# Causal mask and row maximum of attention: from mask products on TensorE to one VectorE instruction

## The chip, the cores and the metric

One core of a Trainium2 chip runs a whole decoder layer. The metric is the device time of one execution in microseconds (us). The time before is the median of 3 runs, 1476.31 us (1475.5 to 1485.98). Engines: TensorE (PE) multiplies matrices, VectorE (DVE) does elementwise work and reductions, ScalarE (ACT) activations, GpSimd (POOL) masks and indirect DMAs, SyncE (SP) issues most DMAs.

## The reference

Four batches of 512 tokens of width 512 pass through attention with 16 heads of 32, a quantised linear unit, and a mixture of 16 experts, with a layer norm behind each. What matters here is attention:

```python
scores = jnp.einsum('bsnh,btnh->bnst', k, q) / math.sqrt(HEAD_SIZE)
scores = jnp.triu(scores) + -10000.0 * jnp.tril(ones, k=-1)
attn = jax.nn.softmax(scores, axis=2)
out = jnp.einsum('bnkq,bknh->bqnh', attn, v)
```

It is causal: a query sees the keys up to its own place. The softmax needs, for each query, the largest score over those keys.

## The kernel before

Attention is computed one batch after another, each in a pass over a list of steps written out by hand (`SEQ`, lines 164 to 173). The first pass holds attention of batch 0 alone. Three more passes, a loop, hold attention of batch i merged with the quantised unit and the routing of batch i-1 ("fused passes"). A last pass holds the rest of batch 3 with the first shared-expert tiles (from some 600 us), and after it come the shared and routed experts. Every engine walks the same list, each doing its own part of every step.

The steps of a head h (0 to 15), all with float32 operands:

- `max:h` finds the row maxima. For each block q of 128 queries (4 blocks) PE takes the next of the three banks `psR`, and multiplies 128 queries with their first 256, 256, 384 and 512 keys (line 1171; the narrowest product is 256 wide, of which 128 columns are used). A second product (line 1173) adds the mask of the diagonal block: the identity as weights and a 128x128 bf16 tile `mask_qk` with -1e30 above the diagonal, accumulated on the last 128 columns. It signals `s_rfull`. DVE waits for that and takes the negated maximum over 128, 256, 384 or 512 columns into one column of `nm` (line 1566). Its end signals `s_dfree`, which frees the bank.
- `rows:n`, after each four heads: PE transposes 16 columns of `nm`, DVE splits the result in two parts (lines 1569 and 1571), SP stores them as rows 96 and 97 of `qst` (lines 691 and 692).
- `scores:h` computes the scores transposed, with the negated maxima as two more contraction rows, into `psST`: four products of 512, 256, 384 and 256 columns (line 1185). ACT takes the exponential (line 943), POOL zeroes the masked triangle of the result (line 789). So the causal mask of the output comes from POOL; the mask in `max:h` touches the maximum alone.
- `weigh:h` multiplies by the values and sums the denominators (lines 1202 and 1206).

The three banks `psR` go round in ticket order over all steps that use them: a step may write a bank when the step three tickets ahead has been evacuated, by DVE (`s_dfree`) or ACT (`s_afree`). So a `max` head takes four tickets, and PE can be at most three blocks ahead of DVE. The order around the heads in a fused pass: `max:0 max:1`, two transposes, `max:2`, two transposes, `max:3`, then `xs:0` and `xq:0` (quantisation on DVE, lines 1481 to 1497) beside `qk:4`, `qk:5`, `v:3` on PE; `scores:0` and transposes, then `max:4`, `max:5`, `max:6` with transposes and `scores` between them, `h:0` products, `max:7`; later `max:8` to `max:11`, and `max:12` to `max:15` with `scores:8` to `scores:10` between. The keys and queries of heads 4g to 4g+3 come through a DMA from `scr_d` (line 687), which waits until `scores` of the group two before (4g-8 to 4g-5) has read the same buffer.

POOL builds the constants at the start (lines 738 to 768). PE waits for all 15 of them (line 1098), DVE too.

Of the kernel before, what the change touches and what calls it, by code (L numbers as in the profile page):

```python
# [7 lines left out]
BF16 = mybir.dt.bfloat16  # L8
I32 = mybir.dt.int32
U32 = mybir.dt.uint32  # L10
ALU = mybir.AluOpType
ACT = mybir.ActivationFunctionType
AX = mybir.AxisListType

P = 128
# [6 lines left out]
NEG = -1e30  # L22
BIG = 1e30
# [11 lines left out]
def decoder_layer(nc, x, fside, ctxw, Wqkv, bqkv, Wo, bo, gate_w, ebias, w1, w2, w3, sw1, sw2, sw3, out):  # L35
    B, S, D = x.shape
    C = D // P
    ST = S // P
    I2 = ctxw.shape[2]
    C2 = I2 // P  # L40
    E, _, F = w1.shape
    NT = B * ST
# [13 lines left out]
    with ExitStack() as ctx:  # L56
        def sb(name, shape, dt=F32, stack=ctx):
            return stack.enter_context(nc.sbuf_tensor(name, shape, dt))
# [4 lines left out]
        ident = sb("ident", [P, P])  # L63
        identb = sb("identb", [P, P], BF16)
        ones = sb("ones", [P, P])
        mask_qk = sb("mask_qk", [P, P], BF16)
        hot = sb("hot", [P, 4, 32])
        sel = sb("sel", [P, C, P])
        tri16 = sb("tri16", [P, E, E])
        tri4 = sb("tri4", [P, 4, 4])  # L70
        upper = sb("upper", [P, P])
        k128 = sb("k128", [P, E, NT])
        jrow = sb("jrow", [P, P, 1])
        krow = sb("krow", [P, TOPK, E])
        halfp = sb("halfp", [P, 8])
# [39 lines left out]
        s_rfull = sem("s_rfull")  # L115
# [72 lines left out]
        def apart(eng):  # L188

            eng.sem_inc(s_apart, 1)  # L190
# [141 lines left out]
        nm = sa("nm", [P, HEADS, ST])  # L332
# [395 lines left out]
        def _(pool):  # L728
            n = [0]

            def fill(t, v):
                pool.memset(t, v).then_inc(s_pool_fill, 1)
                n[0] += 1

            def cut(t, pattern, base, mult, op, v):
                pool.affine_select(out=t, in_=t, compare_op=op, fill=v, base=base, pattern=pattern,
                                   channel_multiplier=mult).then_inc(s_const, 1)
            fill(ident[:, :], 0.0)
            fill(identb[:, :], 0.0)
            fill(ones[:, :], 1.0)  # L740
            fill(mask_qk[:, :], 0.0)
            fill(hot[:, :, 0:4], 0.0)
            fill(hot[:, :, 4:32], 1.0)
            fill(sel[:, :, :], 0.0)
# [6 lines left out]
            cut(ident[:, :], [[-1, P]], 0, 1, ALU.not_equal, 1.0)  # L751
            cut(identb[:, :], [[-1, P]], 0, 1, ALU.not_equal, 1.0)

            cut(mask_qk[:, :], [[-1, P]], 0, 1, ALU.is_ge, NEG)
            cut(hot[:, :, 0:4], [[1, 4], [-1, 4]], 0, 0, ALU.not_equal, 1.0)
            for j0 in (0, 2):
                cut(sel[:, :, HD * j0:HD * (j0 + 2)].rearrange("p n (j r) -> p n j r", r=HD), [[-1, C], [-HD, 2], [0, HD]],
# [212 lines left out]
        def _(pe):  # L970
# [135 lines left out]
            def walk(steps, a, b, at):  # L1106
# [6 lines left out]
                for x in steps:  # L1113
# [8 lines left out]
                    kind, n = x[0], (x[1] if len(x) > 1 else None)  # L1122
# [31 lines left out]
                    if kind in ONE:  # L1154
                        t = at.take_bank(pe, x)
# [9 lines left out]
                    elif kind == "max":  # L1165

                        i, j = n // 4 % 2, n % 4
                        for q in range(ST):
                            t = at.take_bank(pe, x, q)
                            w = max(2, q + 1) * P  # L1170
                            pe.matmul(t[:, 0:w], qst[0:96, i, j, q * P:(q + 1) * P], kst[0:96, i, j, 0:w],  # L1171
                                      start=True, stop=False)
                            pe.matmul(t[:, q * P:(q + 1) * P], identb[:, :], mask_qk[:, :], start=False,  # L1173
                                      stop=True).then_inc(s_rfull, 1)
                    elif kind == "rows":
                        mm = pe.transpose(t[0:4 * ST, 0:P], nm[:, 4 * n:4 * n + 4, :].rearrange("p h q -> p (h q)"),
                                          ident[:, :])
                    elif kind == "scores":

                        i, j = n // 4 % 2, n % 4  # L1180
                        for kb in (0, 3, 1, 2):
                            if n and kb in (0, 3):
# [3 lines left out]
                                           start=True, stop=True)  # L1186
                            if kb in (0, 2):
                                mm.then_inc(s_st, 1)
                    elif kind == "weigh":
# [9 lines left out]
                        for kb in ((1, 2, 3) if part else (0,)):  # L1199
# [4 lines left out]
                            for h, j in pair:  # L1204
                                q0 = HD * quad(j)
                                mm = pe.matmul(psDEN[q0:q0 + HD, kb * P:S], hot[:, g, :], pT[:, h % 4, cols],  # L1206
                                               start=(g == 0 and kb == 0), stop=(g == C - 1 and kb == ST - 1),
# [36 lines left out]
        def _(dve):  # L1244
# [196 lines left out]
            def walk(steps, a, b, at):  # L1441
                k = [0]
                asked = [0]
                x = None
# [9 lines left out]
                def done(ins):  # L1454
                    ins.then_inc(s_dfree, 1)
# [79 lines left out]
                for x in steps:  # L1535
                    kind, n = x[0], (x[1] if len(x) > 1 else None)
# [26 lines left out]
                    elif kind == "max":  # L1563
                        for q in range(ST):
                            dve.wait_ge(s_rfull, at.ticket(x) + (q + 1))
                            done(dve.tensor_reduce(nm[:, n, q:q + 1], at.bank(x, q)[:, 0:(q + 1) * P], AX.X, ALU.max,  # L1566
                                                   negate=True))
                    elif kind == "rows":
                        made(dve.tensor_copy(nmh[:, n % 2, :], t[0:4 * ST, 0:P]))
                        after()  # L1570
# [143 lines left out]
```

## Time and profile before

| | us |
|---|---|
| median of 3 runs | 1476.31 |
| lowest, highest | 1475.5, 1485.98 |
| the profiled execution | 1484.92 |
| its span, first to last instruction | 1483.2 |
| TensorE busy in the span | 1339.3 |
| VectorE busy in the span | 888.9 |

The profile shows one execution. Outside the span lie 1.7 us. Durations of matmuls run from start to a modelled end, and successive ones overlap, so what a matmul costs its engine is read from start to start.

### The profile page before, as it was taken

How to read it: one execution, taken by the hardware profiler on the slowest of the kernel's cores; microseconds unless marked ns; L12 is line 12 of the kernel's file. 1: busy time of each engine (PE TensorE's matmuls, PEld its weight loads, DVE VectorE, ACT ScalarE, POOL GpSimd, SP SyncE). 2: the span in 40 equal slices, each digit the busy share in tenths (PEclk: the TensorE clock that was granted, in tenths of full speed). 3: DMA queues.
4: the chain of work that ended last, by engine and by line, in shares of the span. 5: the costliest groups of instructions: out<-in, count | busy, mean ns of one | idle time of the engine just before them, and what ended most of it. 6: DMA issues, size and time to landing. Idle time of an engine off the chain costs nothing.

```text
span 1483.2 us, 24661 instructions
## 1 busy us (share of the span) xinstructions
PE 1339.3 (90%) x7339; PEld 992.9 (67%) x7339; DVE 888.9 (60%) x1579; ACT 411.6 (28%) x627; POOL 389.5 (26%) x478
## 2 busy tenths in 40 slices
PE   7988998999998998789978998999999999879991
PEld 3553455445454455278857887999999999768890
DVE  2542787669856887687757876334343455555634
ACT  1132133303341144212120013223222334343423
POOL 1131012200230014000001671344444344343432
PEclk9989998999989999889998999999999999999996
DMA  8431533225420632413110012645464456868437
GB/s 283 133 89 39 156 92 96 72 87 141 114 72 23 176 100 68 154 39 131 58 57 29 29 37 66 167 77 139 77 141 75 84 133 140 236 175 237 83 72 249
DMA packets 90109, 163.96 MB, mean 111 GB/s; under 512 B 8544, under 2 KB 29536, under 8 KB 89968
## 3 DMA queue, kind: packets, MB, share of 16 engines
q1 hardware_dynamic: 73168, 122.88, 26.7%
q0 software_dynamic: 16816, 39.59, 14.4%
q8 instruction: 57, 0.93, 0.3%
q14 instruction: 68, 0.56, 0.1%
HBM read 113.42 MB, written 49.02 MB: 110 GB/s over the span
## 4 chain that ended last, share of the span: by engine, by line
PE 68%; DVE 11%; DMA 7%; issue 7%; ACT 2%; SPq 1%; POOL 1%; DVEq 1%; ACTq 0%; POOLq 0%
PE psUA L1001 13%; PE psUB L1001 12%; PE psR L1095 11%; PE psY L1008 9%; PE psR L1008 5%; PE psR L1171 3%; PE psOT L1202 3%; PE psST L1185 3%; PE psTX L984 2%; PE psR L1109 2%; DMA kst<-scr_d 2%; PE psTH L1017 2%; DMA room<-in_L_ffn_w_dram 2%; DMA qst<-nml 1%; DVE nm L1566 1%
## 5 line engine op out<-in xcount | busy, mean ns | idle before, releaser
L1001 PE MATMUL psUA<-w_s,xgT 128*128 (+1 forms) x1284 | 244.6, 341 | 18.8 <-DVE xgT L1379 16.1
L1001 PEld LDWEIGHTS psUA<-w_s,xgT 128*128 128x128 f32 x1284 | 214.4, 196 | 27.0 <-DVE xgT L1379 15.4
L1001 PE MATMUL psUB<-w_s,xgT 128*128 (+1 forms) x1284 | 225.3, 324 | 0.0
L1001 PEld LDWEIGHTS psUB<-w_s,xgT 128*128 128x128 f32 x1284 | 211.4, 190 | 0.0
L827 POOL DMA_INDIRECT sx_d<-yg,dst_i x74 | 119.4, 1614 | 299.3 <-ACT yg L905 261.8
L867 ACT ACTIVATE silg<-psUA 128x352 f32<-128x352 f32 x107 | 49.6, 464 | 432.8 <-PE psUB L1001 432.8
L1008 PE MATMUL psY<-w_s,hgT 128*128 (+3 forms) x621 | 163.6, 408 | 0.1
L789 POOL TENSOR_SCALAR_AFFINE_SELECT pT<-pT 128x128 f32<-128x128 f32 (+1 forms) x192 | 68.5, 375 | 347.6 <-ACT pT L943 347.5
L1388 DVE SCALAR_TENSOR_TENSOR hg<-silg,cws,psUB 128x352 f32<-128x352 f32 x75 | 43.5, 579 | 174.4 <-ACT silg L867 174.4
L1566 DVE TENSOR_REDUCE nm<-psR 128x1 f32<-128x128 f32 (+3 forms) x256 | 113.1, 486 | 41.9 <-PE psR L1173 37.5
L1008 PEld LDWEIGHTS psY<-w_s,hgT 128*128 128x128 f32 (+1 forms) x621 | 114.6, 192 | 23.0 <-DVE hgT L1396 0.5
L1095 PE MATMUL psR<-xT,room 128*128 128x512 f32 x256 | 116.9, 603 | 2.5 <-ACT xT L915 2.5
L1394 DVE CAST hgT<-psTH 128x384 fp32r<-128x384 f32 x107 | 59.5, 556 | 93.7 <-PE psTH L1017 93.2
L814 POOL DMA_INDIRECT xg<-x_d,src_i x77 | 98.3, 1277 | 54.1 <-issue 22.2
L943 ACT ACTIVATE pT<-psST 128x512 f32<-128x512 f32 (+1 forms) x128 | 84.3, 703 | 89.3 <-PE psST L1185 88.0
L1171 PE MATMUL psR<-kst,qst 96*128 96x256 f32 (+2 forms) x256 | 94.3, 439 | 16.2 <-DMA kst<-scr_d 6.5
L1259 DVE TENSOR_TENSOR w_s<-room,w_s (+2 forms) x54 | 88.2, 1668 | 32.3 <-ACT w_s L858 29.8
L1095 PEld LDWEIGHTS psR<-xT,room 128*128 128x128 f32 x256 | 48.0, 193 | 59.2 <-issue 54.2
L1202 PE MATMUL psOT<-pT,v_s 128*32 128x256 f32 (+3 forms) x512 | 81.1, 443 | 7.3 <-POOL pT L789 7.3
L1008 PE MATMUL psR<-w_s,hgT 128*128 (+1 forms) x333 | 86.8, 405 | 0.8 <-issue 0.8
L858 ACT CAST w_s<-room (+2 forms) x54 | 73.6, 1404 | 46.6 <-DMA room<-in_L_ffn_w_dram 20.1
L1206 PE MATMUL psDEN<-pT,hot 128*32 128x256 f32 (+3 forms) x512 | 80.9, 443 | 0.0
(218 smaller groups left out, 1901.3 us busy)
## 6 DMA issues: line engine op xcount, KB each, us to landing
room<-in_L_ffn_w_dram SPq DMA_DIRECT2D x32, 704.0 KB
scr_d<-qhl SPq DMA_DIRECT2D x32, 512.0 KB, 3.7
qst<-scr_d SPq DMA_DIRECT2D x48, 256.0 KB, 4.0
kst<-scr_d SPq DMA_DIRECT2D x48, 256.0 KB, 5.9
room<-in_L_ffn_w_dram SPq DMA_DIRECT2D x16, 512.0 KB
xt<-in_x_dram SPq DMA_DIRECT2D x5, 1024.0 KB, 7.2
xr<-in_x_dram SPq DMA_DIRECT2D x4, 1024.0 KB, 5.5
breg<-in_fside_BxS2xS_dram SPq DMA_DIRECT2D x4, 1024.0 KB, 7.1
```

The source lines that it names most:

```text
L814: pool.indirect_dma_start(xg[:, 1 + par, :], None, x2_d, bass.IndirectOffsetOnAxis(ap=src_i[:, j:j + 1], axis=0)).then_inc(s_gat[par], 16)
L827: pool.indirect_dma_start(sx_d, bass.IndirectOffsetOnAxis(ap=dst_i[:, j:j + 1], axis=0), yg[:, par, :], None, compute_op=ALU.add).then_inc ...
L858: act.copy(hi, raw).then_inc(s_whi, 1)
L943: act.activation(pT[:, h % 4, lo:hi], psST[:, lo:hi], ACT.Exp, scale=SCALE).then_inc(s_exp, 1)
L1001: mm = pe.matmul(t[:, 0:F], xgT[:, par, a_, c * P:(c + 1) * P], w[:, buf, b_, c, :], start=(c == 0 and n == 0), stop=(c == C - 1 and n == ...
L1008: mm = pe.matmul(psy[:, :], hgT[0:kn, a_, k * P:(k + 1) * P], w2_s[0:kn, buf, b_, k, :], start=(first and k == 0 and n == 0), stop=(last_ ...
L1095: mm = pe.matmul(out_, l, r, start=(n == 0), stop=(n == len(pairs) - 1))
L1171: pe.matmul(t[:, 0:w], qst[0:96, i, j, q * P:(q + 1) * P], kst[0:96, i, j, 0:w], start=True, stop=False)
L1202: pe.matmul(psOT[HD * j:HD * (j + 1), kb * P:S], v_s[:, kb, h * HD:(h + 1) * HD], pT[:, h % 4, cols], start=(kb == 0), stop=(kb == ST - 1) ...
L1206: mm = pe.matmul(psDEN[q0:q0 + HD, kb * P:S], hot[:, g, :], pT[:, h % 4, cols], start=(g == 0 and kb == 0), stop=(g == C - 1 and kb == ST ...
L1259: dve.tensor_tensor(lo, raw, hi.bitcast(F32), ALU.subtract).then_inc(s_wlo if n in UP else s_w2lo, 1)
L1566: done(dve.tensor_reduce(nm[:, n, q:q + 1], at.bank(x, q)[:, 0:(q + 1) * P], AX.X, ALU.max, negate=True))
```

## The change

The masking product on TensorE goes. VectorE adds a mask row and takes the maximum in one instruction, `tensor_tensor_reduce`: out = (scores + mask) * -1, written back over the scores in the same PSUM bank, and its minimum, started at 1e30, into `nm`. That is the same negated maximum. The mask is now `mask_row`, 512 columns of bf16: zeros with the triangle in the last 128, read from the right end for the width that the block needs. Ahead of each of these instructions `apart(dve)` issues an instruction that only counts up a semaphore, so that the wait for PE sits on that one. To make room, two small constant tables (`tri16`, `k128`) become bf16. The widths, banks, tickets and order of the steps stay.

```diff
-        mask_qk = sb("mask_qk", [P, P], BF16)
+        mask_row = sb("mask_row", [P, ST * P], BF16)
-        tri16 = sb("tri16", [P, E, E])
+        tri16 = sb("tri16", [P, E, E], BF16)
-        k128 = sb("k128", [P, E, NT])
+        k128 = sb("k128", [P, E, NT], BF16)
...
-            fill(mask_qk[:, :], 0.0)
+            fill(mask_row[:, :], 0.0)
...
-            cut(mask_qk[:, :], [[-1, P]], 0, 1, ALU.is_ge, NEG)
+            cut(mask_row[:, S - P:S], [[-1, P]], 0, 1, ALU.is_ge, NEG)
...
                             pe.matmul(t[:, 0:w], qst[0:96, i, j, q * P:(q + 1) * P], kst[0:96, i, j, 0:w],
-                                      start=True, stop=False)
-                            pe.matmul(t[:, q * P:(q + 1) * P], identb[:, :], mask_qk[:, :], start=False,
-                                      stop=True).then_inc(s_rfull, 1)
+                                      start=True, stop=True).then_inc(s_rfull, 1)
...
                             dve.wait_ge(s_rfull, at.ticket(x) + (q + 1))
-                            done(dve.tensor_reduce(nm[:, n, q:q + 1], at.bank(x, q)[:, 0:(q + 1) * P], AX.X, ALU.max,
-                                                   negate=True))
+                            apart(dve)
+                            t = at.bank(x, q)[:, 0:(q + 1) * P]
+                            done(dve.tensor_tensor_reduce(t, t, mask_row[:, S - (q + 1) * P:S], -1.0, BIG, ALU.add, ALU.min,
+                                                          nm[:, n, q:q + 1]))
```

## Rows read from the trace of the kernel before

**Rows 1.** The page: busy time by engine, the chain, the group of the maxima

```profile
PE 1339.3 (90%) x7339; PEld 992.9 (67%) x7339; DVE 888.9 (60%) x1579; ACT 411.6 (28%) x627; POOL 389.5 (26%) x478
...
PE 68%; DVE 11%; DMA 7%; issue 7%; ACT 2%; SPq 1%; POOL 1%; DVEq 1%; ACTq 0%; POOLq 0%
...
L1566 DVE TENSOR_REDUCE nm<-psR 128x1 f32<-128x128 f32 (+3 forms) x256 | 113.1, 486 | 41.9 <-PE psR L1173 37.5
```

**Rows 2.** Groups by form (busy us, mean ns of one | idle before): TensorE's mask product

```profile
L1173 PE MATMUL psR<-mask_qk,identb 128*128 128x128 bf16 x256 | 62.7, 245 | 0.0
```

**Rows 3.** Timeline of TensorE, first pass (start us, length us): one head, then scores

```profile
60.48 0.28 PE L1171 MATMUL psR<-kst,qst 96*128 96x256 f32 x1
...
61.56 0.23 PE L1173 MATMUL psR<-mask_qk,identb 128*128 128x128 bf16 x1
61.60 0.89 PE L1185 MATMUL psST<-qst,kst 98*128 98x512 f32 x4
62.32 0.28 PE L1171 MATMUL psR<-kst,qst 96*128 96x256 f32 x1
```

**Rows 4.** Timeline of TensorE, second pass, at the lower clock

```profile
251.72 1.52 PE L1185 MATMUL psST<-qst,kst 98*128 98x512 f32 x4
253.04 0.41 PE L1171 MATMUL psR<-kst,qst 96*128 96x256 f32 x1
...
255.06 0.63 PE L1109 MATMUL psR<-identb,xq 128*128 128x128 bf16 x4
...
256.77 0.42 PE L1171 MATMUL psR<-kst,qst 96*128 96x256 f32 x1
```

**Rows 5.** Groups by form, VectorE: two widths of the maximum, two kinds with two inputs

```profile
L1566 DVE TENSOR_REDUCE nm<-psR 128x1 f32<-128x512 f32 x64 | 43.7, 683 | 1.2
...
L1557 DVE SCALAR_TENSOR_TENSOR qhl<-psR,bqk,qhl 128x512 fp32r<-128x512 f32 x32 | 23.9, 747 | 35.5 <-ACT qhl L933 35.5
...
L1566 DVE TENSOR_REDUCE nm<-psR 128x1 f32<-128x128 f32 x64 | 18.5, 289 | 33.1 <-PE psR L1173 32.2
...
L1562 DVE TENSOR_TENSOR v_s<-psR,room 128x512 f32<-128x512 f32 x16 | 11.0, 686 | 14.2 <-PE psR L1095 14.2
```

**Rows 6.** Timeline of VectorE: four of its smallest instructions

```profile
744.82 0.38 DVE L1467 BATCH_NORM_AGGREGATE mv<-bn 128x2 f32<-128x6 f32 x4
```

**Rows 7.** Timeline of VectorE: maxima in the first pass and in the second

```profile
59.03 5.42 DVE L1566 TENSOR_REDUCE nm<-psR 128x1 f32<-128x128 f32 x12
...
182.11 3.61 DVE L1566 TENSOR_REDUCE nm<-psR 128x1 f32<-128x128 f32 x8
186.27 1.73 DVE L1566 TENSOR_REDUCE nm<-psR 128x1 f32<-128x128 f32 x4 [0.55 <-PE psR L1173]
...
190.44 2.29 DVE L1481 TENSOR_TENSOR xs<-x,psR 128x2048 f32<-128x2048 f32 x1 [0.16 <-PE psR L1095]
...
205.43 1.73 DVE L1566 TENSOR_REDUCE nm<-psR 128x1 f32<-128x128 f32 x4 [0.32 <-PE psR L1173]
```

**Rows 8.** The chain of waits (start us, us, what) ahead of head 12, second pass

```profile
241.22 6.66 DMA kst<-scr_d
```

**Rows 9.** Timeline of VectorE right behind that

```profile
248.49 1.97 DVE L1566 TENSOR_REDUCE nm<-psR 128x1 f32<-128x128 f32 x5 [1.88 <-PE psR L1173]
```

**Rows 10.** Busy time by stretch: us, engines (instructions), PEclk granted, DMA share, GB/s

```profile
38.98:42.39 3.41, 3.09 (x18) 1.92 (x16) 3.33 (x10) 0.00 (x0) 0.00 (x0) 1.00 0.53 163
42.39:49.22 6.83, 6.83 (x16) 3.63 (x17) 3.53 (x8) 0.00 (x0) 0.00 (x0) 0.50 0.91 214
...
182.34:189.17 6.83, 6.14 (x43) 4.01 (x43) 5.57 (x15) 2.15 (x4) 0.00 (x0) 1.00 0.53 184
250.61:260.85 10.24, 10.24 (x41) 7.61 (x40) 6.36 (x12) 3.88 (x6) 4.36 (x8) 0.50 0.00 1
...
568.40:578.60 10.20, 9.84 (x63) 6.67 (x67) 8.72 (x20) 4.97 (x8) 4.95 (x11) 1.00 0.01 2
```

**Rows 11.** Timeline of GpSimd at the start: a fill of 512 columns

```profile
1.54 0.53 POOL L732 MEMSET sel<- 128x512 f32 x1
```

## The prediction

> **What bounds the kernel now.** Start with the page. TensorE is busy for 90% of the span, VectorE for 60%, and the chain that ended last runs on TensorE for 68% and on VectorE for 11% [rows 1]. So a product taken from TensorE looks like time won. But the change touches only the 64 `max` heads (4 batches, 16 heads), all before 577 us, and there the shares are others. Two questions decide, head by head: how long is a head on TensorE, how long on VectorE, and which of the two do the three banks make the other wait for. The timelines answer that.
>
> TensorE, warm: the head at 60.48 ends where `scores` starts, at 61.60: 1.12 us for eight products. `scores`, four products of 1408 columns, takes 61.60 to 62.32: 0.72 us [rows 3]. The head's four score products also have 1408 columns, so four mask products cost 1.12 - 0.72 = 0.40 us, 0.10 each, though each is shown with 245 ns [rows 2]: products overlap, and only starts count. At the lower clock the head takes 253.04 to 255.06 = 2.02 us and `scores` 1.32: four masks are 0.70 us [rows 4].
>
> VectorE: four maxima are 4 x 486 ns = 1.94 us of busy time [rows 1], but stand in 1.73 us from the first start to the last end [rows 7]: three overlaps of 0.07. Back to back a head takes VectorE 1.94 - 4 x 0.07 = 1.66 us. That is more than TensorE's 1.12. Measured, twelve maxima with `scores` between their heads take 5.42 us, 1.81 a head [rows 7], against 1.12 + 0.72 = 1.84 of TensorE: both engines are nearly full. Two heads back to back take 3.61 us, 1.80 a head; TensorE has time left there and waits for banks, VectorE is the bound. Where two transposes stand between, the next head waits 0.55 us for a bank and its first product. So in much of the `max` work VectorE already sets the pace, and it is VectorE that gets dearer.
>
> **The change, part by part.**
>
> *Taken off TensorE.* 256 mask products with their weight loads: 256 x 0.10 = 26 us if all were on the path and warm. That is the most the change can give, 1.7% of the time (a little more with the three cold stretches). Where VectorE is the bound it gives only latency: the score product now signals itself, and the data are ready sooner by something below the 0.10 us that a mask costs. I take 0.07.
>
> *Added on VectorE.* The trace has no instruction with two inputs and a reduction, and none that writes PSUM. Call d what one of the 256 adds, start to start. By the nearest rows: with 512 columns out of PSUM the maximum shows 683 ns, an add of two inputs 686, a three-operand instruction 747 [rows 5]. So a second input costs nothing, a second operation with a scalar 0.06. If the per-partition result is written by a further small instruction, four of the smallest take 0.38 us, below 0.10 each [rows 6]. Low end: d = 0, if it streams as a plain reduction; below nothing is excluded, since it reads and writes more. Middle: 0.06 + 0.06 = 0.12. High end: between 128 and 512 columns the maximum grows from 289 to 683 ns [rows 5], 1.03 ns a column; the mean width is 320, and if reading and writing one bank made each column cost twice, d would be 0.33. I take d = 0.12, the value nearest to the rows of instructions that do the same arithmetic.
>
> The Trainium skill ("VectorE: DVE Perf Modes", section "Two Vector instructions with no wait between them") says that an operation which also writes out its accumulator is two instructions, the main one and an accumulator read. No row here shows one. By that rule rival 1 below would fall, and the time would be the forecast's or more; it speaks against this change.
>
> *The counting instruction ahead of it* does no work on the engine. While VectorE is behind, TensorE's signal has long come, and the busy instruction before covers it. Where VectorE waits for a head's first block it can add up to 0.1 us (by [rows 6]). Behind it on VectorE stand only the maxima that would have waited too. I set it off against the 0.07 us won above.
>
> *Head by head.* With d = 0.12 a head takes VectorE 1.66 + 0.48 = 2.14 us, TensorE 0.72. Now VectorE is the bound of nearly every `max` stretch.
>
> First pass. Heads 0 to 3, back to back: 1.66 to 1.80 becomes 2.14 twice, the two at the lower clock gain a little: +0.5. Heads 4 to 7, pace 1.84: two steps of +0.3, the one with `weigh` gains 0.2: +0.4. Heads 8 to 11: `max` and other TensorE work mixed, -0.3. Heads 12 to 15: 12 to 13 back to back, +0.4; the other two have a cold TensorE in front of an idle VectorE, 0.7 and more won each with the masks: -1.2 in all with the 0.4. Sum -0.6.
>
> Each fused pass. Heads 0 to 3 stand ahead of the large VectorE work of `xs:0` at 190.44 [rows 7]; VectorE is busy 5.57 of 6.83 us there [rows 10] and the holes of 0.55 are waits for a bank that VectorE itself frees, so they stay. 16 x 0.12 = 1.9, less 0.1 of bank wait that closes between the back-to-back heads, less three holes shortened by 0.07: +1.5. Heads 4 to 6: VectorE idles 0.32 a head [rows 7], 0.48 added: a step of 2.07 becomes 2.14, with head 7 and what `h:0` behind it takes up, +0.2. Heads 8 to 11: TensorE wins some, VectorE loses some, and at the end the load of the next keys (6.66 us [rows 8]) covers both: VectorE idles 1.88 us before head 12 [rows 9]. Here 0. Heads 12 to 15: in passes two and three at the lower clock (0.50 from 250.61 to 260.85 [rows 10]). The pace is 256.77 - 253.04 = 3.73 us [rows 4], far above 2.14, so the 0.70 goes in full three times, less 0.4 at 12 to 13: -1.7. In pass four the clock is 1.00 [rows 10], and there the pace is set near 2.2 either way: 0. Sums: 0, 0, +1.7.
>
> *Start.* The filled mask is 512 columns wide; such a fill took 0.53 us [rows 11], the old one less, and PE waits for all constants: +0.3. The two bf16 tables are used a few times in all: nothing.
>
> Together -0.6 + 0 + 0 + 1.7 + 0.3 = +1.4, taken as +2 with some waits of the counting instruction. The profiled execution took 1484.92 and would take 1487. It stands 8.6 us above the median of 1476.3, so for a median I forecast 1478.
>
> **How it hangs on d.** Up to 0.12 about 105 of the 256 sit where each adds its own d (27 in a fused pass, 24 in the first); above it nearly all bounds move to VectorE, 130 or more. So d = 0 gives 1478 - 105 x 0.12 = 1465; d = 0.3 gives 1478 + 130 x 0.18 = 1501.
>
> **Rivals.**
>
> 1. *The new instruction streams as the old one* (d at most 0.03). For it: the second input is free by [rows 5]. Against: the per-partition result and the scalar operation. Time 1465 to 1469.
>
> 2. *The new instruction is slow* (d from 0.23). One mechanism: it reads and writes the same bank, or waits for its own end before the result is written. VectorE then needs 2.6 to 3.0 us a head, `max` becomes the slowest step of every pass, and heads 8 to 11 outgrow the cover of 1.88 us [rows 9]. For it: no row shows a VectorE write into PSUM. Against: no two-input row is slower than a copy. It decides from d = 0.23, where 130 x 0.11 = 14 us come on top. At 0.33: 1478 + 27 = 1505.
>
> 3. *The clock.* The granted clock was 1.00 in 38.98 to 42.39, when TensorE did back-to-back heads with waits, and 0.50 from 42.39 on; a similar stretch in the second pass, 182.34 to 189.17, kept 1.00 [rows 10]. With the mask products gone and VectorE slower, TensorE streams 1408 columns a head instead of 1920, in longer time,, and could fall to 0.50 in each pass, also in 568.40 to 578.60, which was warm [rows 10]. The price: a pace of 3.73 instead of some 2.2 cost 1.5 us a head for about three heads; one more such stretch in the fourth pass and a shorter one behind heads 0 to 3 of each fused pass make 4.5 + 3 x 1.2 = 8 us: 1486. Against: while VectorE bounds, a slow TensorE costs nothing. The skill's page "TensorE: Matmul & The Clock Gate" (section "What's actually happening") says that the default state is throttled and activity releases it; by that rule work taken away can slow what is left. The fall at 42.39 agrees, the stretch in the second pass shows that it need not come.
>
> **Chances.** Forecast (d 0.05 to 0.2, 1471 to 1488) 0.42; rival 1: 0.17; rival 2: 0.26; rival 3: 0.15. One per cent, 15 us, is about what a measurement of this kernel tells from no change. Faster by over 1% needs d near 0 and a warm clock, half of rival 1 and a little of the rest: 0.13. Slower by over 1%: rival 2 and some of rival 3: 0.30. Same: 0.57. Range 1463 to 1506: rival 1 and rival 2 to d = 0.33.
>
> **What would show it.** The group of the maxima keeps 256 instructions, and its mean rises from 486 to about 550 to 610 ns; above 720 is rival 2. TensorE has 256 products fewer, a warm head takes 0.72 us from its start to `scores`. In 181 to 190 us VectorE's idle falls and `xs:0` starts some 1.5 us later after the pass's start; in the cold stretches the pace falls from 3.73 to about 3.0. TensorE's idle time behind `nm` grows. The forecast is wrong if the heads 4 to 6 keep a pace under 1.9 us (then d is small), or if the row of clocks shows 0.50 in new places.

## The result and the profile after

The change made the kernel slower. Four runs of it have a median of 1507.41 us (1501.98 to 1510.09), against 1475.9 us for four of the kernel before: a ratio of 1.0194, 95% interval 1.0141 to 1.0248 (it is the ratio of the means, 1506.7 and 1478.0; the medians alone give 1.021). The same kernel run again later, six runs against 23, gave 1505.47 against 1481.56 us, 1.0156 (1.0126 to 1.0185). So the change costs 1.6 to 1.9%.

| us | before | after |
|---|---|---|
| median | 1475.9 | 1507.41 |
| the profiled execution | 1484.92 | 1507.82 |
| its span | 1483.2 | 1506.1 |
| TensorE's mean granted clock | 0.954 | 0.934 |

The page of after, the same three lines as in [rows 1]:

```profile
PE 1351.6 (90%) x7075; PEld 990.2 (66%) x7083; DVE 902.3 (60%) x1835; ACT 412.7 (27%) x627; POOL 393.3 (26%) x478
...
PE 67%; DVE 12%; issue 8%; DMA 6%; ACT 3%; POOL 1%; SPq 1%; DVEq 1%; ACTq 1%; POOLq 0%
...
L1566 DVE CUSTOM_DVE_ANT_0 psR<-psR,mask_row 128x128 f32<-128x128 f32 (+3 forms) x256 | 121.5, 513 | 43.5 <-PE psR L1171 40.8
```

TensorE lost its 256 products (7339 to 7075 records, a few are missing) and is still busy 12 us longer; more of its products ran at the lower clock, where a score product of 256 columns is shown with 0.41 us and not 0.28 ([rows 3], [rows 4]). VectorE gained 256 instructions and only 13 us. Neither share of busy time says where 23 us went.

To see where, cut the span at the four reciprocals of the denominators, one at the end of each attention pass: 123.21, 280.44, 440.64 and 596.74 us before, 124.38, 286.62, 454.24 and 621.32 after. Busy time by stretch, with columns as in [rows 10], of before and then of after:

```profile
0.00:123.21 123.21, 108.44 (x568) 57.96 (x568) 42.96 (x87) 31.70 (x48) 26.91 (x83) 0.92 0.53 163
123.21:280.44 157.23, 143.50 (x753) 76.73 (x754) 110.15 (x214) 44.14 (x69) 26.26 (x56) 0.96 0.33 95
280.44:440.64 160.20, 148.06 (x765) 77.32 (x764) 120.50 (x238) 46.22 (x72) 26.19 (x56) 0.96 0.34 96
440.64:596.74 156.10, 143.81 (x765) 74.10 (x764) 119.76 (x238) 45.84 (x72) 26.48 (x56) 0.99 0.34 97
```

```profile
0.00:124.38 124.38, 105.93 (x504) 54.09 (x504) 45.58 (x151) 31.70 (x48) 27.27 (x83) 0.93 0.54 162
124.38:286.62 162.24, 145.16 (x687) 75.22 (x690) 113.25 (x278) 44.36 (x69) 26.76 (x56) 0.92 0.32 92
286.62:454.24 167.62, 152.65 (x699) 76.77 (x700) 123.79 (x302) 46.46 (x72) 26.37 (x56) 0.90 0.32 95
454.24:621.32 167.08, 151.59 (x699) 75.89 (x700) 124.37 (x302) 46.38 (x72) 26.36 (x56) 0.91 0.31 88
```

The passes grew by 1.2, 5.0, 7.4 and 11.0 us, 24.6 together, and what follows took 886.5 us before and 884.8 after. The loss is all in attention, and in the three fused passes the granted clock fell from 0.96, 0.96 and 0.99 to 0.92, 0.90 and 0.91.

**What the new instruction costs.** Groups by form, VectorE, after (busy us, mean ns of one | idle before), beside [rows 5]:

```profile
L1566 DVE CUSTOM_DVE_ANT_0 psR<-psR,mask_row 128x512 f32<-128x512 f32 x64 | 46.1, 721 | 1.1
...
L1566 DVE DVE_READ_ACCUMULATOR2_ANT nm<- 128x1 f32 x256 | 35.8, 140 | 0.3
...
L1566 DVE CUSTOM_DVE_ANT_0 psR<-psR,mask_row 128x128 f32<-128x128 f32 x64 | 19.6, 306 | 34.5 <-PE psR L1171 34.4
```

It is two instructions: a main one of 306 to 721 ns (289 to 683 before) and 256 accumulator reads of 140 ns that write `nm`. The Trainium skill says so ("VectorE: DVE Perf Modes", section "Two Vector instructions with no wait between them"), and this trace agrees. What it costs VectorE is read where nothing waits. Timeline of after, VectorE, first pass:

```profile
62.82 0.60 DVE L1566 CUSTOM_DVE_ANT_0 psR<-psR,mask_row 128x384 f32<-128x384 f32 x1
...
63.33 0.14 DVE L1566 DVE_READ_ACCUMULATOR2_ANT nm<- 128x1 f32 x1
63.33 0.73 DVE L1566 CUSTOM_DVE_ANT_0 psR<-psR,mask_row 128x512 f32<-128x512 f32 x1
...
63.98 0.14 DVE L1566 DVE_READ_ACCUMULATOR2_ANT nm<- 128x1 f32 x1
64.08 0.30 DVE L1566 CUSTOM_DVE_ANT_0 psR<-psR,mask_row 128x128 f32<-128x128 f32 x1
```

The accumulator read of one block lies beside the main instruction of the next: both start at 63.33. From start to start the 384 columns take 0.51 us here. Over all back-to-back pairs the shortest such steps, by width, were 0.197, 0.330, 0.463 and 0.597 us before, and 0.206, 0.349, 0.482 and 0.616 after. So d, what one block adds to VectorE's throughput, is 0.01 to 0.02 us.

What it costs a wait is something else. Timelines of before and then of after, the first block of head 4 in the second pass:

```profile
202.50 0.23 PE L1173 MATMUL psR<-mask_qk,identb 128*128 128x128 bf16 x1
...
202.77 0.29 DVE L1566 TENSOR_REDUCE nm<-psR 128x1 f32<-128x128 f32 x1 [0.55 <-PE psR L1173]
```

```profile
206.38 0.37 PE L1171 MATMUL psR<-kst,qst 96*128 96x256 f32 x1
...
206.94 0.30 DVE L1566 CUSTOM_DVE_ANT_0 psR<-psR,mask_row 128x128 f32<-128x128 f32 x1 [0.75 <-PE psR L1171]
207.16 0.14 DVE L1566 DVE_READ_ACCUMULATOR2_ANT nm<- 128x1 f32 x1
```

Before, the product ends at 202.73 and VectorE starts 0.04 us later; its bank is free at 203.06, 0.29 after the start. After, the product ends at 206.75, VectorE starts 0.19 later, and the bank is free when the accumulator read is over, at 207.30, 0.36 after the start. The signal that frees the bank hangs on the accumulator read in this trace. Over the 256 blocks the least start behind the end of the block's product is 37 ns before and 189 ns after. VectorE waited so for TensorE in more than the first block of a head: 136 of the 256 maxima of before start within 0.06 us of their product's end, and 103 of after within 0.20. The median from start to free bank goes from 291, 424, 549 and 681 ns (by width) to 358, 492, 640 and 788. A block that TensorE and VectorE hand to each other takes 0.15 + 0.07 = 0.22 to 0.15 + 0.11 = 0.26 us longer to come back. The table of waits shows TensorE waiting for banks (what waits <- for what: us in all, times, longest; gaps under 0.15 us are not in it). Of before, then of after:

```profile
PEld psR L1171 <- DVE nm L1566: 11.2, 30, 1.1
```

```profile
PEld psR L1171 <- DVE nm L1566: 38.3, 88, 1.7
```

Not all of this rise is a loss. The experiments below have 25.9 us in this row with the mask product gone and nothing else changed (e1), 31.3 with the counting instruction too (e5), and 12.0 with the counting instruction and the product (e3).

### The profile page after: what moved, and what is told of

It reads as the page before. It is cut to its first block, busy times and chain, and to the rows that moved or that the text cites. A ratio compares the mean times of both kernels' runs of the same rounds, so it can differ in the third digit from the quotient of the medians.

```text
span 1506.1 us, 24653 instructions
## 1 busy us (share of the span) xinstructions
PE 1351.6 (90%) x7075; PEld 990.2 (66%) x7083; DVE 902.3 (60%) x1835; ACT 412.7 (27%) x627; POOL 393.3 (26%) x478
## 4 chain that ended last, share of the span: by engine, by line
PE 67%; DVE 12%; issue 8%; DMA 6%; ACT 3%; POOL 1%; SPq 1%; DVEq 1%; ACTq 1%; POOLq 0%
PE psUA L1001 13%; PE psUB L1001 12%; PE psR L1095 12%; PE psY L1008 8%; PE psR L1008 4%; PE psR L1171 4%; PE psOT L1200 3%; PE psST L1183 3%; PE psR L1109 3%; PE psTX L984 2%; PE psTH L1017 2%; DMA room<-in_L_ffn_w_dram 2%; DMA kst<-scr_d 2%; DMA qst<-nml 1%; DVE w_s L1257 1%
## 5 line engine op out<-in xcount | busy, mean ns | idle before, releaser
L1566 DVE CUSTOM_DVE_ANT_0 psR<-psR,mask_row 128x128 f32<-128x128 f32 (+3 forms) x256 | 121.5, 513 | 43.5 <-PE psR L1171 40.8
L1095 PE MATMUL psR<-xT,room 128*128 128x512 f32 x256 | 123.2, 630 | 2.4 <-ACT xT L915 2.4
L1200 PE MATMUL psOT<-pT,v_s 128*32 128x256 f32 (+3 forms) x512 | 85.8, 464 | 7.4 <-POOL pT L789 7.4
L1171 PEld LDWEIGHTS psR<-kst,qst 96*128 96x128 f32 x256 | 50.2, 222 | 62.7 <-DVE nm L1566 38.3
```

The costliest lines, as they stand in the source:

```text
L1095: mm = pe.matmul(out_, l, r, start=(n == 0), stop=(n == len(pairs) - 1))
L1200: pe.matmul(psOT[HD * j:HD * (j + 1), kb * P:S], v_s[:, kb, h * HD:(h + 1) * HD], pT[:, h % 4, cols], start=(kb == 0), stop=(kb == ST - 1) ...
L1566: done(dve.tensor_tensor_reduce(t, t, mask_row[:, S - (q + 1) * P:S], -1.0, BIG, ALU.add, ALU.min, nm[:, n, q:q + 1]))
```

## The experiments

Three things changed at once: the mask product went, a counting instruction came, and the maximum became the fused instruction. The first runs ask what each does alone, the later ones what the clock has to do with it. Runs e1 to e4 shared one chip, e5 to e8 a second and e9 to e12 a third, each beside runs of the kernel before; from one group to another only the ratios are compared. The ratios are not taken from the medians, and differ by up to 0.2% from the quotients of the medians.

| run | median us (lowest to highest) | ratio to before (95%) | us of attention at 0.50 |
|---|---|---|---|
| e1_product_gone | 1481.19 (1475.91 to 1487.32) | 0.999 (0.9964 to 1.0017) | 75 |
| e3_count_before | 1492.89 (1486.06 to 1499.1) | 1.0071 (1.0041 to 1.01) | 68 |
| e5_gone_count | 1489.96 (1481.92 to 1496.2) | 1.0065 (1.0032 to 1.0099) | 75 |
| e2_both | 1508.4 (1506.04 to 1516.17) | 1.0172 (1.0119 to 1.0225) | 92 |
| e4_filler_ahead | 1507.47 (1495.65 to 1509.69) | 1.0148 (1.008 to 1.0217) | 89 |
| e6_warm_before | 1480.79 (1473.51 to 1491.77) | 1.0011 (0.9986 to 1.0036) | 31 |
| e7_warm_gone | 1480.83 (1476.53 to 1490.73) | 1.0006 (0.9983 to 1.0029) | 62 |
| e8_warm_after | 1503.33 (1502.24 to 1505.34) | 1.0158 (1.0129 to 1.0187) | 79 |
| e9_short_filler | 1481.82 (1466.45 to 1487.98) | 0.9986 (0.9958 to 1.0014) | 48 |
| e10_gone_filled | 1476.94 (1471.38 to 1484.36) | 0.9962 (0.9941 to 0.9982) | 41 |
| e11_after_again | 1505.47 (1500.89 to 1514.89) | 1.0156 (1.0126 to 1.0185) | 126 |
| e12_after_filled | 1500.9 (1496.26 to 1511.4) | 1.0125 (1.0082 to 1.0168) | 72 |

The last column adds up the stretches at a granted clock of 0.50 before the last reciprocal, in each run's profile; it is 51 us in the kernel before and 109 in the profile of after.

### The parts alone

**e1_product_gone**: the kernel before without the mask product; the maximum is the plain one. It leaves the mask out of the maximum alone (a row's maximum is then taken over the whole diagonal block); e5, e7 and e10 leave out the same.

```diff
-                                      start=True, stop=False)
-                            pe.matmul(t[:, q * P:(q + 1) * P], identb[:, :], mask_qk[:, :], start=False,
-                                      stop=True).then_inc(s_rfull, 1)
+                                      start=True, stop=True).then_inc(s_rfull, 1)
```

> The kernel before without the mask product, VectorE's plain maximum kept (the mask is left out of the maximum alone; POOL still masks the result). Clock theory (TensorE with fewer columns between its waits is granted the lower clock, and that is where the 31 us went): the gain of up to 26 us is eaten by cold stretches, granted clock 0.945 or lower, time 1470 to 1490. VectorE theory (the new instruction and its start are the cost): no such cost here, so the products' time comes out as won, 1460 to 1468, clock near 0.954.

Measured: 0.999, and a mean granted clock of 0.946 over the ten runs against 0.955 over those of before. This is about what the clock theory had stated (0.945 or lower, 1470 to 1490 us); the VectorE theory's 1460 to 1468 us did not come. Taking 256 products away gives nothing that can be told from nothing. One reason stands in the table of waits of e1, beside the 11.2 us of before:

```profile
PEld psR L1171 <- DVE nm L1564: 25.9, 71, 1.5
```

TensorE is done sooner and waits for the bank that VectorE frees: this wait grew by 15 us, where the products could give 26 at most. The other reason is the clock: in the profile the second pass has 13.7 us at 0.50 in both kernels and is 3.9 us shorter in e1 (153.37 against 157.23), while the fourth has 20.5 us at 0.50 against 3.4 and is 4.3 us longer (160.38 against 156.10). The section on the clock puts a size on it.

**e2_both**: the kernel after, with a second product of zeros on TensorE, so that its work is that of before.

```diff
                             pe.matmul(t[:, 0:w], qst[0:96, i, j, q * P:(q + 1) * P], kst[0:96, i, j, 0:w],
-                                      start=True, stop=True).then_inc(s_rfull, 1)
+                                      start=True, stop=False)
+                            pe.matmul(t[:, q * P:(q + 1) * P], identb[:, :], mask_row[:, 0:P], start=False,
+                                      stop=True).then_inc(s_rfull, 1)
```

> The changed kernel with a second product kept on TensorE, identity times a tile of zeros, in the place of the mask product; VectorE does the fused instruction. Clock theory: TensorE streams what it did before, the clock is back at 0.95, time 1480 to 1490. VectorE theory: VectorE is as in the changed kernel and TensorE has more to do, 1505 to 1515.

Measured: 1.0172, where the kernel after had 1.0194 and 1.0156, and within what the VectorE theory had stated. The product's return cannot be told from nothing at these intervals (half a per cent either way), so the loss is there with VectorE's part alone.

**e3_count_before**: the kernel before, with the counting instruction ahead of each maximum. **e5_gone_count**: the same in e1.

```diff
                             dve.wait_ge(s_rfull, at.ticket(x) + (q + 1))
+                            apart(dve)
                             done(dve.tensor_reduce(nm[:, n, q:q + 1], at.bank(x, q)[:, 0:(q + 1) * P], AX.X, ALU.max,
                                                    negate=True))
```

> The kernel before with the counting instruction ahead of each plain maximum. It prices the later start of VectorE alone: if the instruction behind a wait of its own starts 0.1 us later, it shows where VectorE waits for TensorE. VectorE theory: a good part of the loss, 1484 to 1492. Clock theory: near nothing by itself, 1476 to 1481, clock 0.95.

> The first experiment (mask product gone, plain maximum; the mask is left out of the maximum) with the counting instruction ahead of each maximum: all that the changed kernel does but the fused instruction itself. Start-latency theory (the counting instruction costs most): 1492 to 1504, near the changed kernel. Fused-instruction theory (a second small instruction and the later release of the bank): 1483 to 1491, so that the fused instruction makes the larger half of what separates it from the changed kernel.

Measured: e3 1.0071 over before, and e5 1.0065 / 0.999, 0.75% above e1. An instruction that does no work and shows no busy time costs 10 to 11 us, the lower clock that comes with it included (0.951 in e3, 0.955 before). Timeline of e3, the same block as above:

```profile
209.45 0.23 PE L1173 MATMUL psR<-mask_qk,identb 128*128 128x128 bf16 x1
209.83 0.29 DVE L1567 TENSOR_REDUCE nm<-psR 128x1 f32<-128x128 f32 x1 [0.72 <-PE psR L1173]
```

The product ends at 209.68, VectorE starts at 209.83: 0.15 us where before had 0.04, with the same maximum behind it. The least such start is 147 ns in e3, 148 in e5. So of the 0.15 us later start after the change, 0.11 comes with the counting instruction, and 0.04 with the fused one, which also frees its bank 0.07 to 0.11 later. From e5 (1.0065) to the kernel after (1.0156) is the fused instruction alone (with the clock that it brings): 0.9%, with intervals that lie apart. e5's 1489.96 us lies in the range of the fused-instruction theory.

The hand-over can also be seen with the clock out of it. Timelines of TensorE, the first score products of heads 5 and 6, in stretches that have the granted clock at 1.00 throughout; the second pass of before, e1, e3 and after, and the third of e5, in this order:

```profile
205.04 0.28 PE L1171 MATMUL psR<-kst,qst 96*128 96x256 f32 x1
...
207.11 0.28 PE L1171 MATMUL psR<-kst,qst 96*128 96x256 f32 x1
```

```profile
205.17 1.17 PE L1171 MATMUL psR<-kst,qst 96*128 96x256 f32 x4
...
207.23 0.52 PE L1171 MATMUL psR<-kst,qst 96*128 96x256 f32 x2
```

```profile
212.55 0.28 PE L1171 MATMUL psR<-kst,qst 96*128 96x256 f32 x1
...
214.82 0.28 PE L1171 MATMUL psR<-kst,qst 96*128 96x256 f32 x1
```

```profile
209.62 0.28 PE L1171 MATMUL psR<-kst,qst 96*128 96x256 f32 x1
...
212.22 0.28 PE L1171 MATMUL psR<-kst,qst 96*128 96x256 f32 x1
```

```profile
367.37 1.28 PE L1171 MATMUL psR<-kst,qst 96*128 96x256 f32 x4
...
369.66 0.52 PE L1171 MATMUL psR<-kst,qst 96*128 96x256 f32 x2
```

The step is 2.07 us before, 2.06 without the product, 2.27 and 2.29 with the counting instruction, 2.60 with the fused one too. At this place the product is worth nothing, the counting instruction costs 0.2 us a head and the fused one 0.3. Elsewhere the product is worth something: from head 0 to head 1 of the second pass, at 1.00 in both, it is 182.94 - 181.05 = 1.89 us before and 181.43 - 179.70 = 1.73 in e1.

### The clock

Without the products the granted clock fell in new places. The next questions were whether TensorE's missing work is the cause, and how much of the loss comes through it.

**e4_filler_ahead**: the kernel after, with a product that nothing reads ahead of each score product, in the same bank, so that TensorE has its old work but the score product itself still signals.

```diff
                             w = max(2, q + 1) * P
+                            pe.matmul(t[:, 0:P], identb[:, :], mask_row[:, 0:P], start=True, stop=True)
                             pe.matmul(t[:, 0:w], qst[0:96, i, j, q * P:(q + 1) * P], kst[0:96, i, j, 0:w],
```

> The changed kernel with a filler product (identity times zeros, 128 columns) ahead of each score product, overwritten by it, so that VectorE is signalled by the score product itself. Clock theory: as with the second product kept, clock 0.95, time 1478 to 1490. VectorE theory: 1500 to 1512.

Measured: 1.0148, within the interval of the kernel after. Like e2 it gives TensorE its work back and the time doesn't change beyond the intervals. Attention has 89 us at 0.50 in e4 and 92 in e2, more than the 51 of before, though TensorE's products are as many. Over all runs the mean granted clock is 0.955 before, 0.946 with the products alone gone (e1), 0.946 and 0.945 with VectorE's part beside as many products (e4, e2), and 0.937 with both (after). So the missing products and VectorE's part each lower it.

**e6_warm_before, e7_warm_gone, e8_warm_after**: three products of 512 columns that nothing reads, ahead of head 12, where TensorE waits for the load of the keys ([rows 8]); in the kernels before, e1 and after.

```diff
+                        if n == 12:
+                            idle = at.take_bank(pe, x, 0)
+                            for _ in range(3):
+                                pe.matmul(idle, ident[:, :], sel[:, :, :].rearrange("p c n -> p (c n)"), start=True, stop=True)
+                            apart(pe)
```

> The kernel before with three filler products (float32, 512 columns, 1.3 us) in the wait for the keys ahead of head 12, where TensorE is idle. It touches the clock alone. Clock theory: the stretch at 0.50 behind head 12 (10 us in each of the first three passes) is gone or shorter, 3 to 5 us won in each: 1468 to 1478, granted clock 0.96. If the clock costs nothing there: no change or +1 to +3.

> Mask product gone, plain maximum, and the same filler ahead of head 12. Clock theory: here the products' time comes out as well: 1460 to 1474, ratio 0.985 to 0.995. If the clock is not what ate the gain: as the first experiment, 0.997 to 1.001.

> The changed kernel with the same filler ahead of head 12. Clock theory: 5 to 12 us off its time, 1495 to 1503; the cold stretches behind heads 1 to 3 of the fused passes stay. VectorE theory: 1505 to 1510, no change.

Measured: 1.0011, 1.0006 and 1.0158, no gain in any. They didn't do what was meant. Timeline of e7:

```profile
247.58 2.84 PE L1148 MATMUL psR<-sel,ident 128*128 128x512 f32 x6
```

Each float32 product of 512 columns is two instructions, and the three take 2.8 us, twice what was reckoned. In e6 the step from head 11 to head 12 of the second pass grew from 7.1 to 9.7 us, while heads 12 to 15 went from 8.8 to 6.5: the clock was won and its worth given back at once. So these three runs don't say what the clock is worth.

**e9_short_filler** has one such product instead of three, in the kernel before. **e10_gone_filled** is e1 with this and, in heads 0 to 3, a product of 256 columns ahead of the last score product. **e12_after_filled** is the kernel after with the fillers of e10.

```diff
+                        if n == 12:
+                            pe.matmul(at.take_bank(pe, x, 0), ident[:, :], sel[:, :, :].rearrange("p c n -> p (c n)"),
+                                      start=True, stop=True)
+                            apart(pe)
...
+                            if n < 4 and q == 3:
+                                pe.matmul(t[:, 0:2 * P], ident[:, :], sel[:, 0:2, :].rearrange("p c n -> p (c n)"),
+                                          start=True, stop=True)
```

> The kernel before with one filler product in place of three ahead of head 12. A float32 product is two instructions, so three took 2.6 us, twice what was meant, and made head 12 late; one takes 0.9 and fits the wait of 1.3. Clock theory: head 12 is on time, heads 12 to 15 warm in more passes, 1470 to 1477, ratio below 1. If it is too short to hold the clock: as before, 1478 to 1484.

> Mask product gone, plain maximum, one filler ahead of head 12 and one of 256 columns ahead of the widest block of heads 0 to 3, where VectorE is two blocks behind. Clock theory: the cold stretches behind heads 2 and 3 of the first experiment go as well, and the products' time comes out, 1462 to 1472. Otherwise 1478 to 1483.

> The changed kernel itself, beside the others on one chip, to set the fifth experiment (1.0065 without the fused instruction) against it on more runs of before: 1.015 to 1.020. The fused instruction by itself is then worth 0.9 to 1.3%.

> The changed kernel with the fillers of the tenth experiment (one product ahead of head 12, 256 columns ahead of the widest block of heads 0 to 3). It parts the clock from VectorE's longer waits. If the clock is all of the loss: ratio 1.000 to 1.005. If it is about half, as the cold time of the profiles says (58 us more, at some 0.4 us each 23 us, of which the fillers take away half): 1.006 to 1.012. If VectorE's waits are nearly all: 1.014 to 1.018.

Measured: e9 0.9986, not told from no change; e10 0.9962 (0.9941 to 0.9982), the only version that beats both kernels, if by 0.4%, though above the 1462 to 1472 us of its clock theory; e11 1.0156; and e12 1.0125, whose value fell between what two theories had stated. Busy time by stretch, the whole of attention, of e1, e5, e12 and e11 in this order:

```profile
0.00:595.15 595.15, 536.40 (x2593) 275.02 (x2594) 392.02 (x774) 168.17 (x258) 106.50 (x251) 0.94 0.38 110
```

```profile
0.00:601.50 601.50, 538.27 (x2593) 272.26 (x2594) 393.06 (x775) 167.65 (x259) 105.68 (x251) 0.94 0.38 110
```

```profile
0.00:616.65 616.65, 552.95 (x2633) 281.09 (x2634) 407.15 (x1030) 168.11 (x258) 106.29 (x251) 0.94 0.37 107
```

```profile
0.00:629.13 629.13, 561.97 (x2593) 282.19 (x2594) 408.22 (x1031) 168.59 (x259) 107.01 (x251) 0.90 0.36 105
```

The first three have the same clock, 0.94 (75, 75 and 72 us at 0.50), and no mask product. The counting instruction is 601.50 - 595.15 = 6.4 us between e1 and e5. The 616.65 - 601.50 = 15.2 us from e5 to e12 are the fused instruction and e12's fillers together, and fillers are work of their own, so this is not the price of the fused instruction at an equal clock. On the whole the fillers bring 1.0156 - 1.0125 = 0.3%, and from e1 to e10 again 0.3%; in both pairs the intervals overlap, so this gain is not shown.

The single executions give a better scale for the clock. Every execution but the first four of before has its span and mean granted clock listed, and 2 x (1 - clock) x span is its time at 0.50, in attention and behind it. The same program varies from one execution to the next in both, and those with more time at 0.50 are longer, in each of the 16 groups of runs. Over these 179 executions, each measured from the mean of its own group, a microsecond at 0.50 goes with 0.34 us more (0.31 to 0.37). The rows agree: from head 14 to head 15 the kernel before takes 3.73 us at 0.50 in the second pass and 574.65 - 572.38 = 2.27 at 1.00 in the fourth, 1.46 us or 0.39 of the 3.73. With 0.34 each kernel's mean time can be set to one clock. This is an estimate and no experiment: it takes what holds between executions of one program to hold between programs, and it can't tell whether the clock makes a run longer or something else does both.

| kernel | executions | mean us | mean us at 0.50 | mean set to 133 us at 0.50 (estimate) |
|---|---|---|---|---|
| before | 77 | 1481.7 | 132 | 1482 |
| e1, product gone | 10 | 1481.2 | 159 | 1473 |
| e3, counting instruction | 10 | 1492.9 | 147 | 1488 |
| e5, product gone, counting | 6 | 1489.7 | 164 | 1479 |
| after | 10 | 1507.2 | 189 | 1488 |
| e2, after with a second product | 4 | 1509.8 | 167 | 1498 |
| e10, e1 with fillers | 12 | 1477.6 | 124 | 1481 |
| e12, after with fillers | 6 | 1501.4 | 145 | 1498 |

At one clock the mask product is worth some 10 us (before to e1, and e2 to after), the counting instruction costs 6 (before to e3) or 7 (e1 to e5), the fused one 9 (e5 to after), and the fillers cost 8 to 9 themselves (e1 to e10, after to e12). That is -10 + 6 + 9, about 5 or 6 us of the 25.5 between the means. The other 19 or 20 would be the 58 us more at 0.50. So by this estimate most of the loss comes through the clock, and so does most of what e1 did not gain: 9 of its 10 us. What the runs show without it is the whole price of each part with the clock that it brings: nothing for the product, 0.7% for the counting instruction, 0.9% for the fused one.

Two runs would have taken the parts further apart and were not tried: the wait on the fused instruction itself, without the counting one, and the fused output in SBUF instead of the bank, for which there is no room.

## Why the prediction was right and wrong

The forecast was 1478 us, no measurable change, with a chance of 0.57; slower had 0.30, and slower it was. 1507.41 lies 1.4 us above the upper end of the range; the later median of 1505.47, and 1476.31 x 1.0194 = 1505, lie just within it. The direction was among the rivals and the likeliest case was wrong. That the range reached so far is luck: it did so for a dear instruction (rival 2), which the new one is not.

- **The most that TensorE could give, 26 us.** The products gave nothing (e1 has 0.999). The reading behind it, that VectorE and the banks set the pace, is half of the reason: the wait for banks grew by 15 us, and the estimate above has 10 us won at an equal clock and 9 lost through the clock, which the forecast left to rival 3. VectorE's own pace was also put too high: 1.66 us a head, where the shortest steps add up to 0.197 + 0.330 + 0.463 + 0.597 = 1.59, and 136 of 256 maxima start straight on TensorE's signal. "VectorE is the bound" was too strong; often it was the trip between the two.
- **d, taken 0.12 us.** It measured 0.01 to 0.02. The bounds held (0 to 0.33) but the choice didn't: the two 0.06 were taken from operations whose own durations are longer, and the small second instruction, put "below 0.10", measured 140 ns but lies beside the next block. So the second instruction that the Trainium skill's rule made the prediction expect is there, and the inference that rival 1 would fall by it isn't borne out. The group's mean rose to 513 ns, or 653 with the read, neither in the 550 to 610 forecast. Rival 1's condition (d at most 0.03) was met and its 1465 to 1469 us did not come; rival 2's (d from 0.23) was not, and its 1505 did. The argument that hung all cases on d had the wrong variable.
- **The failing step is the wait, and the clock behind it.** The prediction put the counting instruction at up to 0.1 us and set it off "against the 0.07 us won above". It measured 0.11, and e3 shows that alone to cost 0.7%. Nothing was put down for a later start of the fused instruction (0.04) or for the later release of the bank (0.07 to 0.11). The sentence that behind the waiting instruction stand "only the maxima that would have waited too" was the slip: with three banks TensorE waits for the release, so a delay goes round. The step from head 5 to head 6 shows it at 1.00: 2.06, 2.29, 2.60 us. At 0.24 us for a block, the 103 blocks of after that start straight on the signal would make 25 us; the estimate at one clock has 15 to 16 for both instructions, with the product's 10 won against it. The forecast put nothing down for the clock, and after has 58 us more at 0.50, some 20 us by the estimate.
- **Head by head.** Heads 4 to 6: "a step of 2.07 becomes 2.14"; measured 2.60 (after, the second pass, first score products of two heads in a row at 209.62 and 212.22). Timeline of after, the second block of head 4, product and fused instruction:

```profile
207.56 0.38 PE L1171 MATMUL psR<-kst,qst 96*128 96x256 f32 x1 [0.82 <-ACT xqT L917]
...
208.14 0.43 DVE L1566 CUSTOM_DVE_ANT_0 psR<-psR,mask_row 128x256 f32<-128x256 f32 x1 [0.84 <-PE psR L1171]
```

The product ends at 207.95 and VectorE starts 0.19 us later, though it had stood idle for 0.84 (the product itself had waited for ScalarE). Heads 0 to 3: `xs:0` was to start 1.5 us later after head 0 in the second pass. It was 190.44 - 182.11 = 8.33 us behind it before, and 194.00 - 183.24 = 10.76 after, 2.4 later. VectorE's hole before heads 2 and 3 was to stay or shrink by 0.07, and grew from 0.55 to 0.82. Part of both is the clock: after has 0.50 here from 185.78 on, where before has 1.00. Timeline of after:

```profile
183.24 0.29 DVE L1566 CUSTOM_DVE_ANT_0 psR<-psR,mask_row 128x128 f32<-128x128 f32 x1
...
188.06 0.30 DVE L1566 CUSTOM_DVE_ANT_0 psR<-psR,mask_row 128x128 f32<-128x128 f32 x1 [0.82 <-PE psR L1171]
...
194.00 2.29 DVE L1479 TENSOR_TENSOR xs<-x,psR 128x2048 f32<-128x2048 f32 x1 [0.81 <-PE psR L1095]
```

- **The gain in the cold stretches** was forecast as a pace of 3.73 falling to about 3.0. It fell to 262.51 - 259.17 = 3.34 us. In e1, whose release is as quick as before's, the same step takes 410.87 - 407.74 = 3.13 us in the third pass, also at 0.50. So the gain was real there, 0.60 of the 0.70 forecast, and VectorE's part left 0.39 of it. (In the second pass of e1 heads 12 to 15 take 5.6 us instead of 8.8, but at 1.00, which is the clock and not the product.) Timeline of after, TensorE:

```profile
259.17 1.81 PE L1171 MATMUL psR<-kst,qst 96*128 96x256 f32 x4
...
262.51 0.95 PE L1171 MATMUL psR<-kst,qst 96*128 96x256 f32 x3
```

- **Rival 3, the clock** (0.15), named the places and most of the mechanism. It had a stretch behind heads 0 to 3 in each fused pass; all three came, where the profile of before has the same heads at 1.00 (busy time by stretch, after):

```profile
185.78:196.02 10.24, 10.08 (x30) 5.51 (x30) 7.64 (x23) 2.24 (x4) 0.00 (x0) 0.50 0.67 155
349.62:359.86 10.24, 10.04 (x31) 5.69 (x31) 7.63 (x23) 2.15 (x4) 0.00 (x0) 0.50 0.68 159
520.29:530.53 10.24, 9.88 (x26) 5.12 (x23) 7.61 (x20) 1.77 (x4) 0.00 (x0) 0.50 0.66 154
```

  The Trainium skill's rule that activity releases the clock and its default is the throttled state ("TensorE: Matmul & The Clock Gate", section "What's actually happening") agrees (mean granted clock 0.955 before, 0.946 in e1, where only work was taken away). The rival's price of 8 us is too low: the 58 us more at 0.50 are some 20 us by the estimate. Its argument against itself, that a slow TensorE costs nothing while VectorE bounds, isn't borne out by 0.34 us for each microsecond. The sign that the prediction named for itself, 0.50 in new places, came. The clock isn't wholly the change's doing either: e6 and e9, with the mask products and the plain maximum, also have a stretch behind heads 0 to 3 of the second pass (181.8 to 192.0, 183.1 to 193.3), which the profile of before lacks.
- **The sums by pass**: -0.6 (with +0.3 for the start), 0, 0 and +1.7 were forecast; 1.2, 5.0, 7.4 and 11.0 were measured. The fourth pass, at 0.99 before, had the most to lose: 3.4 us at 0.50 became 30.7.

## What to carry to other kernels

Where two engines hand a few banks back and forth, price an edit by its round trip, from the producer's end to the free bank, and not by its busy time or its throughput: here the throughput cost was 0.02 us a block and the round trip 0.24. Before moving work off the engine with the largest busy share, look in the table of waits at what it waits for around that work; if it is the other engine's release, part of the time saved turns into that wait (15 us here). Keep an instruction that only counts a semaphore off a hand-over that waits. And where TensorE's clock moves between its levels, add it to the sum and not beside it: take each run's granted clock with its time, and compare kernels at one clock before calling a part cheap or dear.

## What was not expected of the hardware

- An instruction on VectorE that does no work delays the start behind a wait by 0.11 us (37 to 148 ns) and is not in the busy time at all; 256 of them cost 0.7% of this kernel.
- The fused instruction reads and rewrites its PSUM bank at the pace of a plain maximum (0.616 us from start to start for 512 columns, 0.597 before); in-place output in the bank isn't slow.
- The accumulator read (140 ns) runs beside the next main instruction, so it costs no throughput, but the signal of the fused operation hangs on its end.
- The same program, profiled twice, spent 109 and 126 us of attention at 0.50, and took 621.3 and 629.1 us for it: the clock's stretches differ from run to run, and a single profile carries that with it. Over 179 executions of 13 programs, a microsecond at 0.50 went with 0.34 us of time within each program.
